# The condition's sum moved to a TensorE product, and the last quotient of the first mixing written in token halves

## The reference, cut to what matters

```python
def _bi_wkv(r, k, v, w, u, time_emb):        # r = x, k = v = side input f, time_emb = cond_512 (4 x 64)
    tf = sigmoid(sum(time_emb, axis=-1))[:, None, None]
    decay = exp(-exp(w))[None, :] * (0.5 + 0.5 * tf[:, :, 0])
    ek = exp(minimum(k, 30.0)); ekv = ek * v
    # nf, df: forward scans  a = a * decay + ekv,  b = b * decay + ek;  nb, db: the same backward
    euk = exp(minimum(u + k, 30.0))
    num = nf + nb - ekv + euk * v
    den = df + db - ek + euk
    return sigmoid(r) * (num / maximum(den, 1e-08)) * (0.8 + 0.2 * tf)
x = x + attention(_bi_wkv(x, f, f, w, u, cond_512), w_qkv, ...)
```

## Time and profile before

| | us |
|---|---|
| median of 3 runs | 1454.25 |
| the runs | 1453.51, 1454.25, 1458.26 |
| the profiled execution, its own time | 1452.27 |
| its span, first to last instruction | 1450.5 |
| PE busy | 1365.4 (94%) |
| first matmul starts | 37.33 |
| first scan starts | 10.19 |
| mean granted TensorE clock | 0.99 |

### The profile page before, as it was taken

How to read it: one execution, slowest core, us unless ns; L and a number is a source line. 1 busy time by engine, 2 the same in 40 slices (tenths; PEclk the granted TensorE clock), 3 DMA queues, 4 the chain that set the end, 5 groups by cost and what they waited for, 6 DMA issues and landing times.

```text
span 1450.5 us, 22073 instructions
## 1 busy us (share of the span) xinstructions
PE 1365.4 (94%) x7888; PEld 767.7 (53%) x7888; DVE 1079.7 (74%) x2468; ACT 853.9 (59%) x1745; POOL 462.1 (32%) x375
## 2 busy tenths in 40 slices
PE   0879999999999999999999999988999999999998
PEld 0534754754664574575475476475444444444443
DVE  8898899889789889989988988955599675613000
ACT  4577677678578667767767857755533333212432
POOL 5151161161153135116116115215064343200432
PEclk9999999999999999999999999979999999999999
DMA  3120030030021022003003002102283444100220
GB/s 108 43 94 16 16 124 9 8 116 22 17 76 62 17 66 73 16 16 123 16 2 124 15 17 77 33 17 94 69 232 101 117 128 117 59 0 0 78 97 29
DMA packets 39092, 88.70 MB, mean 61 GB/s; under 512 B 5384, under 2 KB 25352, under 8 KB 37840
## 3 DMA queue, kind: packets, MB, share of 16 engines
q1 hardware_dynamic: 38704, 87.23, 19.5%
q10 hardware_dynamic: 288, 0.14, 0.0%
HBM read 84.77 MB, written 2.59 MB: 60 GB/s over the span
## 4 chain that ended last, share of the span: by engine, by line
PE 68%; DVE 18%; ACT 8%; issue 3%; DMA 2%; POOL 1%; DVEq 0%; ACTq 0%; SPq 0%; POOLq 0%
PE bank L512 13%; PE bank L1812 12%; PE bank L1790 11%; PE bank L1911 5%; DVE m L1179 5%; PE bank L611 4%; PE bank L626 4%; DVE m L1183 3%; PE bank L574 3%; PE bank L541 3%; DVE conv L1082 3%; PE bank L606 2%; PE bank L617 2%; PE bank L628 2%; ACT conv L834 2%
## 5 line engine op out<-in xcount | busy, mean ns | idle before, releaser
L1082 DVE SCALAR_TENSOR_TENSOR conv<-bank,taps,conv 128x510 f32<-128x510 f32 x366 | 270.4, 743 | 27.7 <-ACT conv L820 18.4
L512 PE MATMUL bank<-rT,wf 128*128 128x512 f32 x512 | 253.8, 611 | 6.9 <-DVE conv L1093 4.1
L1662 POOL TENSOR_TENSOR ffn_weighted<-ffn_relu,ffn_wide 128x512 f32<-128x512 f32 x96 | 128.7, 1374 | 299.9 <-DMA ffn_wide<-ffn_shares 148.0
L1812 PE MATMUL bank<-ffn_weighted,feat 128*128 128x512 f32 x400 | 186.8, 595 | 3.8 <-POOL ffn_weighted L1662 3.8
L1790 PE MATMUL bank<-rT,feat 128*128 128x512 f32 x400 | 187.4, 595 | 0.0
L1325 POOL TENSOR_TENSOR sq<-sq,qsq 128x512 f32<-128x512 f32 x64 | 82.9, 1296 | 270.3 <-ACT sq L1008 269.6
L1673 ACT ACTIVATE ffn_relu<-bank 128x512 f32<-128x512 f32 x100 | 59.6, 596 | 182.3 <-PE bank L1790 182.3
L512 PEld LDWEIGHTS bank<-rT,wf 128*128 128x128 f32 x512 | 89.5, 191 | 87.9 <-issue 73.7
L1812 PEld LDWEIGHTS bank<-ffn_weighted,feat 128*128 128x128 f32 x400 | 76.0, 190 | 100.1 <-issue 98.2
L1790 PEld LDWEIGHTS bank<-rT,feat 128*128 128x128 f32 x400 | 76.0, 191 | 93.9 <-issue 93.1
L574 PE MATMUL bank<-rT,wz 128*128 128x512 f32 x256 | 115.3, 604 | 8.9 <-DVE m L1183 6.1
(11 more groups left out here) (235 smaller groups left out, 2612.0 us busy)
## 6 DMA issues: line engine op xcount, KB each, us to landing
z<-decay_rows SPq DMA_DIRECT2D x64, 384.0 KB, 4.0
ffn_wide<-ffn_shares SPq DMA_DIRECT2D x64, 256.0 KB, 5.3
feat<-in_L_chunks_dram SPq DMA_DIRECT2D x25, 512.0 KB, 4.2
wf<-in_wf_dram SPq DMA_DIRECT2D x8, 1024.0 KB, 4.9
wz<-in_wz_dram SPq DMA_DIRECT2D x8, 512.0 KB, 3.6
wo<-in_wo_dram SPq DMA_DIRECT2D x8, 512.0 KB, 3.8
ffn_wide<-ffn_shares SPq DMA_DIRECT2D x8, 512.0 KB, 4.0
m<-in_fT_dram SPq DMA_DIRECT2D x2, 512.0 KB, 5.1
```

Source lines behind the costliest of these rows:

```text
L512: ins = pe.matmul(banks[bank_of(p, n)][:], wf[:, c, ORDER[n // NH], :], rT[:, c, halves(n % NH)], start=(c == 0), stop=(c == CT - 1))
L1082: dve.scalar_tensor_tensor(acc[:, :, k:], src[:, :, 0:T - k], taps[:, ORDER[n // NH], KS - 1 - k:KS - k], acc[:, :, k:], ALU.mult, ALU.add ...
L1662: pool.tensor_tensor(hw[:, j, u, :], h2[:, j, u, :], wide[:, j, u // NH % BLOCKS, halves(u % NH)], ALU.mult).then_inc(weighted, 1)
L1812: last = pe.matmul(banks[4 + 2 * c + h][:], chunk[:, slot, CT + t, c * P:(c + 1) * P], of, start=start, stop=stop, skip_group_check=True)
```

## The change

The condition is loaded transposed, on 64 partitions with 4 numbers each, straight from DRAM with single-number steps. PE multiplies it with a 64 x 128 block of ones, which puts the four sums on all 128 partitions in PSUM bank 7 (`cond_sum`); ACT reads them there. DVE's reduction is gone, and DVE makes the factors ahead of the cuts of the second half instead of behind them. `cond_sum` stands in PE's queue right behind the wait on `consts_in`. The last quotient is written in two token halves, each raising `r_ready` by one, and PE waits for the first half before unit 0 and for the second before unit 1.

```diff
--- before.py
+++ after.py
@@ -89,8 +89,9 @@
     dtb, alog, ga = scratch(NVH), scratch(NVH), scratch(NVH)
     pre, mag, e, l, sp_, g = (scratch(TT, NVH) for _ in range(6))
     grow = scratch(NT)[0:NVH, :]
-    cond = room["cond"][:, 0:B * 64].rearrange("p (b t) -> p b t", b=B)
-    tsum, es, tf, thalf, ew, dw = (room["small"][:, k * 4:k * 4 + 4] for k in range(6))
+    cond = room["cond"][0:64, 0:B]
+    tsum = banks[7][:, 0:B]
+    es, tf, thalf, ew, dw = (room["small"][:, k * 4:k * 4 + 4] for k in range(5))
 
     f_in = [sem(f"f_in{c}") for c in range(CT)]
     wu_in, cond_in, x_in, heads_in = (sem(n) for n in ("wu_in", "cond_in", "x_in", "heads_in"))
@@ -143,7 +144,7 @@
 
     def scalar(act):
         act.dma_start(wu[:], a["wu"]).then_inc(wu_in, 16)
-        act.dma_start(cond, a["cond"].partition_broadcast(P)).then_inc(cond_in, 16)
+        act.dma_start(cond, a["cond"].rearrange("b t -> t b"), allow_slow_non_contiguous=True).then_inc(cond_in, 16)
         act.preload_act_table_set("natural_log_exp_and_others")
 
         def into_bank(c):
@@ -231,6 +232,15 @@
             dve.wait_ge(sig_ready, 1 + B)
             step.issue(dve.tensor_tensor(nf[:, c, :], nf[:, c, :], sig[:, c, :], ALU.mult))
 
+        def quotient_by_halves(c):
+            dve.wait_ge(rec_ready, 2 * c + 2)
+            step.need(step.n)
+            for h in range(NH):
+                x, y = df[:, c, halves(h)], db[:, c, halves(h)]
+                step(dve.tensor_tensor(x, x, y, ALU.mult))
+                step(dve.scalar_tensor_tensor(x, x, 2.0, y, ALU.subtract, ALU.mult))
+                dve.tensor_tensor(rT[:, c, halves(h)], nf[:, c, halves(h)], x, ALU.mult).then_inc(r_ready, 1)
+
         def quotient(c):
             dve.wait_ge(rec_ready, 2 * c + 2)
             step(dve.tensor_tensor(df[:, c, :], df[:, c, :], db[:, c, :], ALU.mult))
@@ -241,11 +251,6 @@
         least(0)
         dve.wait_ge(wu_in, 16)
         least_own(0)
-        dve.wait_ge(cond_in, 16)
-        dve.reduce_sum(tsum, cond, AX_X).then_inc(tsum_ready, 1)
-        dve.wait_ge(f_in[1], 16)
-        least(1)
-        least_own(1)
         dve.wait_ge(decay_exps, 3)
         step(dve.tensor_scalar(tf, es, 1.0, None, ALU.add))
         step(dve.reciprocal(tf, tf))
@@ -253,6 +258,9 @@
         step(dve.tensor_tensor(fac[:].rearrange("p i c b -> p (i c) b"), thalf.unsqueeze(1).to_broadcast([P, 2 * CT, B]),
                                dw.unsqueeze(2).to_broadcast([P, 2 * CT, B]), ALU.mult))
 
+        dve.wait_ge(f_in[1], 16)
+        least(1)
+        least_own(1)
         dve.wait_ge(exps_ready, 1)
         scan(0, df, ek, 1).then_inc(fwd_ready, 1)
         dve.tensor_scalar(tout[:], tf, -0.2, -0.8, ALU.mult, ALU.add).then_inc(tout_ready, 1)
@@ -271,7 +279,7 @@
         step.issue(scan(1, nb, ekv, -1))
         denominator(1)
         numerator(1)
-        quotient(1)
+        quotient_by_halves(1)
 
     def early(dve):
         dve.wait_ge(heads_in, 80)
@@ -287,6 +295,11 @@
         dve.wait_ge(decay_exps, 4)
         step.issue(dve.scalar_tensor_tensor(g, sp_, -1.0, ga.unsqueeze(1).to_broadcast([P, TT, NVH]),
                                             ALU.mult, ALU.mult))
+
+    def cond_sum(pe):
+        pe.wait_ge(consts_set, 1)
+        pe.wait_ge(cond_in, 16)
+        pe.matmul(tsum, ones[0:64, :], cond, start=True, stop=True).then_inc(tsum_ready, 1)
 
     def heads_full(pe, c):
         if c == 0:
@@ -311,7 +324,8 @@
         last.then_inc(sums_full, 1)
 
     return dict(sync=sync, gpsimd=gpsimd, scalar=scalar, gains=gains, soft=soft, take_rows=take_rows, vector=vector,
-                early=early, middle=middle, heads_full=heads_full, sums=sums, r_ready=r_ready, sums_read=sums_read,
+                early=early, middle=middle, heads_full=heads_full, cond_sum=cond_sum, sums=sums,
+                r_ready=r_ready, sums_read=sums_read,
                 store_rows=store_rows, heads_in=heads_in, rows_out=rows_out, COLS_READ=COLS_READ, ROWS_READ=ROWS_READ)
 
 
@@ -780,13 +794,14 @@
             rms(g, NU - 1)
 
         pe.wait_ge(env["consts_in"], 16)
+        front["cond_sum"](pe)
         pe.wait_ge(env["consts_set"], 3)
         pe.wait_ge(front["r_ready"], 1)
         front["heads_full"](pe, 0)
         for n in range(4):
             half(0, n, 0)
-        pe.wait_ge(front["r_ready"], 2)
-        for n in range(2):
+        for n in range(NH):
+            pe.wait_ge(front["r_ready"], 2 + n)
             half(0, n, 1)
         front["heads_full"](pe, 1)
         for n in range(2, 4):
```

## The result

| | before | after |
|---|---|---|
| median of 14 runs each, us | 1456.13 | 1464.76 |
| lowest and highest, us | 1451.87, 1459.15 | 1457.84, 1471.26 |
| ratio to before, 95% interval | | 1.0049 [1.0028, 1.0069] |
| first scan starts, us | 10.19 | 18.47 |
| projection that was released by the convolution, us | 57.20 | 64.91 |

The kernel became slower by 0.49%, about 7 us. The forecast was 1463 in a range of 1459 to 1467. It started from 1454.25 for the kernel before, which stood at 1456.13 in this comparison. Three runs of this study lay far above all others (3472 us of the kernel before, 1630 of e7, 1483 of e6); they are left out of every ratio and fit, while the medians keep them.

What follows compares the result with a forecast made beforehand. The front was taken as one serial line on which PE waits for DVE, its shift carried to the end. +10.1 for the condition and -0.6 for the halves gave +9.5 us on 1454.25: 1463 us, range 1459 to 1467.

Steps and rivals of the forecast that it cites:

- The cause: PE's queue at the start: the condition's product stands behind the wait on consts_in, raised only by the transfer of ident.
- The other queues behind it: Start: ACT's exponential, DVE's factors, cuts and scans, and POOL all wait for the product; POOL moves 9.7, less than the scans.
- The identity's landing, 17.1 +- 0.7: Transfer of ident, SP's eleventh load, issued at 6.20: lands at 17.1 us, at most 0.66 sooner or later from ACT's queue traffic.
- The steps from the landing to the scan: From ident's landing through product, exponential, factors (0.83) and cuts (1.26): first scan at 20.29 us instead of 10.19.
- edit 1: Condition summed by PE's product, at the start of the kernel: first scan later by 10.1 us, bounds 9.4 and 10.8.
- both terms: The front of the kernel: +10.1 us for the condition's sum and -0.6 for the last quotient in halves.
- The halves, -0.6: Last quotient: ACT's first own tap and DVE's convolution start 0.6 us earlier, held by the tap weights' copy; bounds +0.3, -0.8.
- One for one to the end: From the front to the kernel's end: the front's shift in us is carried whole, no fixed-time piece taking it up.
- The rival of a partial take-up: Later in the kernel, slack takes up part of the shift; if half is lost, +4.7 us or 1458; chance 0.09.
- The rival of the not-held product: Start: consts_in raised before about 8 us, scan 1.4 earlier, with the halves -2.0, 1451 to 1452; chance 0.07.
- the rival's other branch: Product not held, but condition landing no sooner than 7.75: cuts end at 11.0, sum about +0.2 us.
- The strided load: Condition's load on ACT's queue: 256 descriptors instead of 128, 0.6 us over 16 engines, under the wait for ident.

Runs made afterwards that it cites:

- e7: e6 with DVE's copy of the tap weights moved ahead of the last numerator; median 1453.93 us, ratio to before 0.9978.
- e6: e5 with the condition loaded from an array the host lays out transposed, 64 rows of 4 numbers; median 1455.04 us, ratio to before 0.9989.
- e3: The changed kernel with PE's product put ahead of the wait for the identity matrix; median 1457.78 us, ratio to before 1.0012.
- e8: The changed kernel with the identity's load issued from ACT's queue right behind the condition's, PE's order kept; median 1456.62 us, ratio to before 1.0007.
- e2: The kernel before with only the last quotient in halves, condition still broadcast and summed on DVE; median 1455.58 us, ratio to before 0.9982.
- e4: e2 with DVE's copy of the tap weights moved from behind the quotient to behind the last denominator; median 1455.34 us, ratio to before 0.9981.
- e5: e3 with the cuts of the second half put back ahead of the factors; median 1453.63 us, ratio to before 0.9987.
- e1: The changed kernel with the last quotient and PE's wait for it as before, so the product only; median 1463.23 us, ratio to before 1.0048.
- e9: e7 with DVE's 4-column instruction making tout moved ahead of the first scan; median 1452.01 us, ratio to before 0.9977.

## Why the prediction was right, step by step

**The cause** (the product behind the identity's load) was right: e3, e8 and the profile's own wait show it. **The other queues behind it** (ACT, DVE, POOL, and the scan as the last of them) too.

**The identity's landing, 17.1 +- 0.7**, was the term that was mis-sized: 15.49. With the condition's broadcast it landed at 17.1 (before), 17.0 (e2) and 16.7 (e4), with single numbers at 15.5 (changed kernel, e5), 15.7 (e1) and 15.9 (e3), with rows of 16 bytes at 14.3 to 14.9 (e6, e7, e9); e8 isn't among them, since its identity is issued elsewhere. The groups don't overlap, so it is the load and not the spread between executions. The side input's second half shows the same: issued at 1.19 in all kernels, it landed at 7.5 to 7.6 with the broadcast and at 5.8 to 6.4 in the eight kernels without it. I had bounded the relief by the packets' own busy time, 0.66 us per engine; from the broadcast to single numbers it was 1.3 between the means, 1.6 between the two profiles of before and after. The broadcast delays what follows by more than the time its packets are counted for; why stays open.

**The steps from the landing to the scan**: release and product 0.26 and 0.46 against 0.04 and 0.59, product's end to ACT 0.04 instead of 0.10, from ACT's start to the factors 0.20 (0.28 forecast), factors 0.84 (0.83 forecast), cuts 1.27 (1.26). The sum from landing to scan was 2.98 against 3.19 forecast. So edit 1 came out at +8.3 instead of +10.1, all but 0.2 of the difference from the landing.

**The size, and some luck.** With both terms at their ends the prediction had +8.6 to +11.1, around +9.5. The front came out at +7.7 and the runs at +7.3 +- 0.8, under that span. The total of 1464.76 lies close to 1463 all the same, because the kernel before stood at 1456.13 in this comparison, 1.9 above the 1454.25 of the forecast, and because the medians differ by 8.6 where the ratio gives 7.1. The mechanism was right; that the forecast time was hit so closely is in part luck.

**The halves, -0.6**: -0.48 in the changed kernel against e1, -0.45 in e2. Six steps took 0.69, 0.72 from start to start. That the tap weights' copy and not PE decides was right, by e4.

**One for one to the end**: 7.7 at the front's end and 7.3 +- 0.8 over the runs. The rival of a partial take-up asked for half to be lost and isn't borne out. On the way the lateness read at single places went down to 5.9 (at 887 us) and up again to 8.2 (at 1018 us). Such steps of 1 to 2 us stand in all profiles here, in both directions, and I did not trace them. The 5 us at 1343 are the fall of the clock that e2, e3, e4 and e8 show as well.

**The rival of the not-held product** priced a kernel that e3 then was, in two branches. The better one, 1451 to 1452, had the first scan at 8.8, set by the cuts alone behind a side input at 7.5. In e3 the side input was there at 6.0, but the condition only at 7.0, and the cuts stood behind the product and the factors: the scan started at 10.01. That is nearer the rival's other branch (condition at 7.75, scan at 11.0, about +0.2 us in all). The measured e3 stands at 1.0012, +0.4 +- 0.8 us at equal clock.

**The strided load**: the Trainium skill ("DMA: Bandwidth & Descriptors", section "Rules for kernel authors") says one descriptor per element. ACT's queue went from 288 packets to 416, which is 128 less and 256 more: this trace agrees. Though they are 1 KB against 128, the single numbers landed hardly sooner than the broadcast: 6.2 to 8.4, 7.6 in the mean of five, against 7.75 in before and 7.7 to 7.8 in e2 and e4.

## What to carry to other kernels

A new instruction inherits every wait that stands ahead of it in its engine's queue. A wait that costs nothing because the engine has nothing to do (here `consts_in` was raised at 17.1 and first needed at 37.33, 20 us later) becomes a bound as soon as something early is put behind it; look up when each of those semaphores is raised, by the transfer's issue and landing, before placing the product. And when a producer is split so that a consumer can start early, list all the things the consumer waits for: here a 0.17 us copy behind the producer kept most of the gain.

## What the runs showed of the hardware that I had not expected

A small DVE instruction can cost 1 us when POOL is at work. `tout` (128 x 4) took 0.25, 1.14, 0.97 and 0.97 us when it came up during POOL's 128 x 1024 product (before, e5, e6, e7; 0.26 in e2 and 0.25 in e4), ending each time 0.02 to 0.03 after it, and 0.14 to 0.17 otherwise (changed kernel, e3, e8, e9); moving it ahead of the product took the cost away (e9). It isn't a wait for the scan's result: in the changed kernel, e3 and e8 it stood right behind the same scans, with POOL's product just over, and took 0.14. The Trainium skill, "SBUF — State Buffer", section "Who interferes with whom", says that a DVE instruction in a two-port mode and POOL exclude each other for a whole instruction, whichever comes first. The waits here agree with that; no trace tells in which mode `tout` ran. The scans beside the same POOL products kept their pace (2.41 for four).

The time of one and the same kernel moved with the mean granted clock, by 1.5 us for each 0.001, between 1449 and 1465 us for the kernel before. A profile of one execution can thus carry 7 us that have nothing to do with a change; places before the first dip can be compared without it (in the profile of before it lies at 100 to 110 us, at 0.66).
